# Two-layer graph attention: GpSimd instead of ScalarE rounds three heads' weighted values, TensorE takes its first unit before a group of transposes, and a few units change hands

## The reference

```python
def layer0(h, adj, W, a):                       # 4 heads, D = 32
    Wh = (h @ W).reshape(N, H, D)               # N = 4096, F = 128
    s_src = einsum('nhd,hd->nh', Wh, a[0, :, :D])
    s_dst = einsum('nhd,hd->nh', Wh, a[0, :, D:])
    e = leaky_relu(s_src[:, None, :] + s_dst[None, :, :], 0.2)
    e = where(adj[:, :, None] > 0, e, -9e15)
    return elu(einsum('ijh,jhd->ihd', softmax(e, axis=1), Wh))

x = layernorm(x + layer0(x, adj, W, a0))
x = layernorm(x + layer1(x, adj, a1))           # one head over 128 features, other norms
```

## Time and profile before

| | |
|---|---|
| time, median of 3 runs | 914.75 us (914.44 to 916.98) |
| the profiled execution | 914.89 us, span 913.1 us |
| PE, DVE, ACT, POOL busy | 839.0, 761.4, 694.4, 43.0 us |
| granted clock of PE, mean | 0.976 |

### The profile page before, as it was taken

The page is one execution under the profiler, slowest core; times in us unless marked ns, Lnnn a source line. Parts: engine busy times, 40 slices in busy tenths (PEclk is TensorE's granted clock), DMA queues, the critical chain, the costliest instruction groups (busy, mean ns, idle before and its releaser), DMA issues.

```text
span 913.1 us, 24394 instructions
## 1 busy us (share of the span) xinstructions
PE 839.0 (92%) x10868; PEld 686.8 (75%) x10868; DVE 761.4 (83%) x1306; ACT 694.4 (76%) x815; POOL 43.0 (5%) x80
## 2 busy tenths in 40 slices
PE   8496999989999889999998898599999999999995
PEld 6496999978999879999998884355555555555552
DVE  3978889899988999889997889775877786878876
ACT  3999998897999989999986994968373654637222
POOL 3200000000000000000000000000000100000000
PEclk9799999999999999999999999799999999999998
DMA  8999377703658227113040002430324453644000
GB/s 146 177 106 249 54 86 77 233 25 35 85 71 197 84 25 86 34 69 143 25 118 19 7 27 68 70 104 13 104 86 159 137 177 104 198 129 153 2 12 14
DMA packets 42065, 84.67 MB, mean 93 GB/s; under 512 B 6242, under 2 KB 31332, under 8 KB 41316
## 3 DMA queue, kind: packets, MB, share of 16 engines
q0 software_dynamic: 12416, 33.56, 26.3%
q1 hardware_dynamic: 29540, 49.50, 15.1%
HBM read 112.27 MB, written 21.12 MB: 146 GB/s over the span
## 4 chain that ended last, share of the span: by engine, by line
PE 50%; ACT 24%; DVE 18%; issue 3%; DMA 3%; POOL 1%; SPq 0%; DVEq 0%; ACTq 0%
PE bank L1299 21%; PE bank L688 18%; ACT ring L620 16%; PE bank L1277 7%; ACT masks L767 3%; DVE ring L653 3%; DVE ring L633 3%; DMA adj_tiles<-in_adj_dram 3%; PE bank L1289 2%; PE bank L536 2%; ACT masks L523 1%; DVE evac L704 1%; DVE ring L657 1%; DVE ring L663 1%; ACT moving L573 1%
## 5 line engine op out<-in xcount | busy, mean ns | idle before, releaser
L688 PE MATMUL bank<-moving,ring 128*128 128x99 bf16 (+1 forms) x6528 | 451.9, 218 | 12.2 <-DVE ring L663 8.8
L688 PEld LDWEIGHTS bank<-moving,ring 128*128 128x128 fp8e4 x6528 | 388.2, 98 | 14.3 <-DVE ring L663 10.0
L620 ACT ACTIVATE ring<-s_rows,scores 128x1024 fp8e4<-128x1024 f32 x372 | 393.1, 1141 | 4.4 <-PE bank L688 3.7
L688 PE MATMUL bank<-moving,masks 128*128 128x99 bf16 x1664 | 222.7, 209 | 18.3 <-DVE evac L704 14.7
L688 PEld LDWEIGHTS bank<-moving,masks 128*128 128x128 fp8e4 x1664 | 163.1, 98 | 20.3 <-DVE ring L657 9.1
L1299 PE MATMUL bank<-moving,masks 128*128 128x387 bf16 x1056 | 178.2, 327 | 0.0
L767 ACT ACTIVATE masks<-s_rows,adj_tiles 128x512 fp8e4<-128x512 f32 x256 | 157.8, 709 | 0.1
L1299 PEld LDWEIGHTS bank<-moving,masks 128*128 128x128 fp8e4 x1056 | 101.7, 96 | 73.0
L653 DVE SCALAR_TENSOR_TENSOR ring<-ring,masks 128x1024 int32<-128x1024 int32 x93 | 113.1, 1217 | 10.9 <-ACT ring L620 10.8
L663 DVE TENSOR_TENSOR ring<-masks,ring 128x1024 int32<-128x1024 int32 x76 | 93.1, 1225 | 26.9 <-PE bank L688 25.2
L395 ACT ACTIVATE ring<-ring 128x4 f32<-128x4 f32 (+1 forms) x24 | 4.9, 205 | 141.0 <-DVE ring L311 115.3
(11 more groups left out here) (214 smaller groups left out, 630.7 us busy)
## 6 DMA issues: line engine op xcount, KB each, us to landing
masks_kept<-masks SPq DMA_DIRECT2D x4, 4096.0 KB, 17.2
masks<-masks_kept SPq DMA_DIRECT2D x8, 2048.0 KB, 9.9
adj_tiles<-in_adj_dram POOLq DMA_DIRECT2D x24, 512.0 KB, 8.5
s_rows<-score_rows SPq DMA_DIRECT2D x14, 512.0 KB, 4.8
ring<-masks_kept POOLq DMA_DIRECT2D x11, 512.0 KB, 3.9
first_part<-masks_kept POOLq DMA_DIRECT2D x11, 512.0 KB, 3.8
second_part<-masks_kept POOLq DMA_DIRECT2D x10, 512.0 KB, 4.0
adj_tiles<-in_adj_dram POOLq DMA_DIRECT2D x16, 256.0 KB, 14.1
```

The costliest lines, as they stand in the source:

```text
L620: last = act.activation(j_tile(below, k), s_rows[:, h % 2, :], ACT.Sign, bias=scores[:, g * JU + k, h:h + 1], saturate=False)
L688: last = pe.matmul(bank[b][:, at + lo:at + hi], mask, moving[:, j, h, lo:hi], start=first, stop=(j == T - 1), skip_group_check=True)
```

## The change

Six roundings of pairs (two parts for each of heads 1 to 3, 12 instructions) leave ScalarE's list for GpSimd's. GpSimd does head 1's after it has issued quarter 3's load, head 2's after the first two tiles of chunk 1 and head 3's after the next two. TensorE turns quarter 1 after unit 0 and no longer before it. In chunk 0 units 6, 11, 19 and 27 get their upper mask from VectorE's XOR; in head 1 VectorE compares two units (9, 12) and no longer three (9, 11, 14), in head 3 it compares 28 in place of 27.

```diff
     ON_ACT = [who == "A" for who in
-              "VAVAAVAA" "AVAVAAVA" "AVAVAAVA" "AVAVAAVA"
+              "VAVAAVAA" "AVAAVAAA" "AVAVAAVA" "AVAAVAVA"
...
     DIRECT = [how == "D" for how in
-              "DDDDDDDD" "DD-D----" "DD-D----" "DD-D----"
+              "DDDDDD-D" "DD------" "DD------" "DD------"
...
+        def round_on_pool(pool, h, q):
+            for b in range(2):
+                pool.wait_ge(cast_asked, 4 * h + 2 * q + b + 1)
+                pool.tensor_copy(all_columns[:, :, h, b, q, :], parts0[b]).then_inc(cast_given, 1)
...
                 for k in range(2, QUARTERS):
                     pool.wait_ge(turned, (k - 1) * (Q // QUARTERS))
                     load_quarter(pool, k)
+                round_on_pool(pool, 1, 0)
+                round_on_pool(pool, 1, 1)
                 for c in range(1, NC):
                     for t in range(CT):
+                        if c == 1 and t in (2, 4):
+                            round_on_pool(pool, 2 + (t - 2) // 2, 0)
+                            round_on_pool(pool, 2 + (t - 2) // 2, 1)
                         if c == 1 and t < AHEAD:
...
-                        if c == 0 and u in (0, 2, 5):
-                            turn_quarter(pe, {0: 1, 2: 2, 5: 3}[u])
+                        if c == 0 and u in (1, 2, 5):
+                            turn_quarter(pe, {1: 1, 2: 2, 5: 3}[u])
...
                         if c == 0 and u < UH:
-                            if u == 2:
-                                round_part(act, 1, 0)
-                                round_part(act, 1, 1)
                             if u == 3:
                                 act_unit(act, c, 3)
                                 act.wait_ge(scores_out, 16)
                                 take_quarter(act, 2)
                             if u == 4:
                                 act_unit(act, c, 4)
-                                round_part(act, 2, 0)
                             if u == 6:
                                 act_unit(act, c, 6)
-                                round_part(act, 2, 1)
                                 take_quarter(act, 3)
-                                round_part(act, 3, 0)
                             if u == 7:
                                 act_unit(act, c, 7)
-                                round_part(act, 3, 1)
```

## The result

The changed kernel takes 922.0 us (median of 6 runs, 921.33 to 923.51) against 914.68 us; the ratio is 1.0078, 95% interval 1.0065 to 1.0091. So it is about 7 us slower; 923.5 was forecast. In its profiled execution the span is 920.7 us, and GpSimd is busy 65.5 us where it was 43.0.

The account below looks back on a forecast made before the run. Bound: ScalarE's list to 83.3 us, TensorE's matmuls to 170, VectorE to 210. Unit 8's AND +12.4, TensorE -3.6, so +8.8 on 914.89: 923.7, by the median 923.5; likeliest case 918 to 928, whole range 908.5 to 928.

Parts of the forecast that it names:

- ScalarE's lead: Head 0: without the roundings ScalarE's list through unit 8 ends at 75 to 77 us, against 83.2; about 8 us.
- Unit 0 at half clock, quarter 1's turns: TensorE: unit 0 runs from 35.5 to 42.35, full clock back at 41.1, quarter 1's turns end at 44.3, against 41.1.
- GpSimd's first rounding: Head 1's rounding stands behind quarter 3's issue (44.3 to 47.2) and begins near 47 us; VectorE waits from 41.6.
- quarter 3's later load: Issued from 44.3, it lands by 62.2 at the latest; TensorE wants it at about 65, so the delay is hidden.
- A rounding's length: 1056 elements on GpSimd: 1.06 us by the MEMSETs' slope, 1.63 by the CAST's own, 1.35 taken.
- Blocking in turn: Likeliest case, 0.55: all twelve GpSimd roundings stand whole in VectorE's time, 12 x 1.35 us; 918 to 928 us.
- The term: Delay of unit 8's AND: 47.2 + 33.4 + 12 x 1.35 = 96.8 against 84.4, 12.4 us later.
- TensorE's 3.6 us: Heads 1 to 3 of chunk 0: units 11, 19 and 27 go from 4.13 to 2.93 us, saving 3.6 us.
- a bound (2.8 us): TensorE's clock: 5.6 us at half clock in front of unit 8 would cost 2.8 us more; not in the sum.
- No mutual blocking: Rival, 0.32: GpSimd and VectorE run side by side, unit 8's AND 2.2 us earlier; 909 to 911 us.
- Partial blocking: Rival, 0.13: only some five roundings that meet a compare, or half of each, block; VectorE loses 4 to 8; 912 to 917.
- the order of TensorE: Unit 0 ahead of quarter 1's turns: ScalarE's second quarter starts at 42.85, not 38.61, and the turns end at 44.3, not 41.1.

Follow-up runs that it names:

- e8: Kernel before plus 12 extra GpSimd copies, then 12 fills, beside VectorE's work: an AND or XOR took 1.94 to 2.05 us beside a copy, 1.22 beside a fill.
- e9: Changed kernel with GpSimd's twelve roundings replaced by fills of the same size that read nothing: 912.7 us, ratio 0.9974.
- e3: Kernel before with only TensorE's order changed (unit 0 ahead of quarter 1's turns): 919.14 us, ratio 1.0052.
- e4: Changed kernel with TensorE's old order (quarter 1's turns ahead of unit 0): 917.08 us, ratio 1.0025.
- e6: Kernel before with only the changed unit tables of heads 1 to 3 of chunk 0, unit 6 staying direct: 912.23 us, ratio 0.9964.
- e1: Kernel before with only the change's two unit tables: 913.64 us, ratio 0.9984.
- e2: Kernel before with only the roundings moved to GpSimd, TensorE's order and both tables as before: 917.41 us, ratio 1.0028.

## Why the prediction was right, point by point

**ScalarE's lead.** Right in kind: unit 8's mask stopped being what unit 8 waits for. In size it was too large: the mask was done at 81.2 and not at 75 to 77, since ScalarE stood 5.8 us for TensorE's turns of quarter 3. It cost nothing, as VectorE came to the AND at 90.8.

**Unit 0 at half clock, quarter 1's turns.** Reckoned 35.5 to 42.35 and turns to 44.3; in the trace 35.95 to 42.47 and to 44.27. The clock was back at about 40.6 (0.68 from 40 to 41 us, then 1.00) where 41.1 was reckoned, which made up for the later start.

**GpSimd's first rounding** was put near 47 and began at 47.42, behind quarter 3's issue. VectorE stood 6.57 us for it. That quarter 3's later load is hidden, held as well: nothing in the chain waits for it.

**A rounding's length.** Put at 1.35 us, between 1.06 and 1.63; it takes 1.07 when undisturbed. So the lower bound was right, the MEMSETs' slope and not the CAST's own share of its short run. For twelve this alone makes 3.4 us of the 4.9 by which unit 8's AND was put too late.

**Blocking in turn.** The step that decided held: e8 and e9 show it. Its ground was weaker than its result: it took the two-operand instructions to be like the compares by their rate of reading, and e8 shows that they are not alike, since a fill holds up the compares and leaves an AND at 1.22 us. Its size was off too: ten of the twelve lengthen a row of VectorE, by 0.74 to 0.95 us, where a whole rounding for each was counted. With what the trace shows the sum is 42.0 (compare of unit 2 done) + 6.6 + 33.4 + 8.6 + 1.0 (a wait for a rounding that was itself held up) = 91.6, and unit 8's AND ended at 91.9. Forecast 96.8. The term was +12.4 and is +7.5.

**TensorE's 3.6 us.** Put in as a gain, and for the most part not received. Units 8 to 11 took 16.63 us; with two direct units and two of 2.93 they should take 14.1. The missing 2.5 us are the clock's, at 0.66 from 90 to 100 us after waits of 6.5 and 3.9 us. The prediction had this as a bound (2.8 us) and left it out of the sum; the kernel before lost only 0.25 us there (15.57 against 15.3). Unit 12 then starts at 110.81 against 102.26, 8.6 us late, unit 24 at 154.95 against 147.19, 7.8, and unit 28 ends at 173.22 against 166.67 (169.60 less one unit of 2.93), 6.6. But the next reduction of VectorE is 7.25 us late again (183.00 against 175.75), since its list bounds that edge, with a compare closer to the end of the chunk and a XOR more. That last point is read from the trace and was not tested by a run. So two sizes were off by about as much in opposite ways, 4.9 us too much and 3.6 us too little, and the total came out 1.5 us high. That the total came so near is luck; the sign, the path through GpSimd's and VectorE's lists, and that the two engines take turns were reasoned out and are borne out.

**The rivals.** No mutual blocking is out by e9: that kernel is what it described (912.7 us, though it was put at 909). Partial blocking is out in kind by the ten long rows: only one of them is a group of compares, and each lost 0.74 to 0.95 us of a rounding of 1.07. In size it was nearer than the whole rounding of 1.35 that the sum had: it allowed VectorE 4 to 8 us, and the rows lost 8.6. That the order of TensorE costs by itself was part of the sum and is shown by e3 and e4.

## What to carry to other kernels

Before work goes to GpSimd, look at what VectorE does meanwhile: beside its instructions with two operands in SBUF, its compares and its fp32 copies, the roundings on GpSimd did not run in parallel. They took turns, and VectorE paid 8.6 us for twelve roundings of 1.07. An engine's list matters as much as its load: GpSimd had stood idle for 14.7 us before quarter 3's issue, and yet VectorE waited 6.6 us for the rounding, since that issue and its wait stood ahead of it in the list. And when one engine's list is shortened, look which other list is the next to bind; here it was VectorE's, and it took the gain.

## What the runs showed of the hardware that was not expected

TensorE's clock does not follow a wait alike each time. In the profiled execution of the kernel before, a wait of 3.81 us in front of unit 8 left it at 1.00:

```profile
86.24 0.20 PE L688 MATMUL bank<-moving,masks 128*128 128x99 bf16 x1 [3.81 <-DVE evac L704]
86.00:88.00 2.00, 1.76 (x28) 1.79 (x29) 1.96 (x5) 2.00 (x3) 0.00 (x0) 1.00 0.92 307
88.00:90.00 2.00, 2.00 (x34) 2.00 (x32) 1.90 (x6) 2.00 (x3) 0.00 (x0) 1.00 0.92 354
```

In e6's, with the same head 0 and the same wait of 3.81 us, it went to half and was back after some 4 us:

```profile
86.00:88.00 2.00, 1.85 (x20) 1.81 (x21) 1.93 (x6) 2.00 (x3) 0.00 (x0) 0.69 0.94 297
88.00:90.00 2.00, 2.00 (x19) 1.88 (x17) 1.93 (x5) 2.00 (x3) 0.00 (x0) 0.50 0.90 252
90.00:92.00 2.00, 2.00 (x33) 1.99 (x31) 1.97 (x3) 2.00 (x3) 0.00 (x0) 0.96 0.65 252
```

e1 and e3 have the same wait of 3.81 us, and in their profiled executions the clock fell as well: units 8 to 11 took 17.19 us in e3 where the same four took 15.57 in the kernel before. What makes the difference is open. It bears on how finely such kernels can be compared by one trace each. It is not the whole spread either: from head 3's reduction to the end, where the work is nearly the same in all of them, the traces take 735.5 us (e1, e2) to 737.7 (the changed kernel), and e1's profiled execution, with its dip, is the fastest of its eleven.
